# Adapter rows laid out in DRAM as the stack has them, and late loads issued in two parts, in a two-layer adapter and expert FFN kernel

## What is computed

```python
# layer 1: W 512x512; adapter of rank 16, picked per tile from 32 slots
y = x @ W.T + b + 2.0 * (x @ A[slot[t]]) @ B[slot[t]]
# layer 2: A2 64x512, router 16x512, experts B2 16x512x64
hidden = y @ A2.T
probs = softmax(y @ router.T)
topw, topi = top_k(probs, 2); topw /= topw.sum() + 1e-6
delta = sum_over_experts(weight[e] * hidden @ B2[e].T)
out = x + y @ W2.T + b2 + 0.5 * delta
```

## Time and profile before

| what | value |
|---|---|
| three runs, median (lowest to highest) | 116.63 us (116.54 to 117.41) |
| the profiled execution, its own time | 116.34 us |
| its span, first to last instruction | 114.6 us |
| so, around the span | 1.74 us |
| mean granted clock of TensorE in it | 0.955 of 2.4 GHz |
| busy share: TensorE, VectorE, ScalarE, POOL | 90%, 55%, 34%, 17% |
| bytes moved by DMA | 17.68 MB, mean 154 GB/s |

### The profile page before, as it was taken

One profiled execution on the slowest core, in us unless ns is written; L12 is line 12 of the kernel. 1 busy time (PEld: TensorE's weight loads), 2 busy tenths in 40 slices (PEclk: granted clock), 3 DMA queues, 4 the chain that ended last, 5 costly groups with the idle time before them and its releaser, 6 DMA issues.

```text
span 114.6 us, 1787 instructions
## 1 busy us (share of the span) xinstructions
PE 103.5 (90%) x577; PEld 92.8 (81%) x577; DVE 62.9 (55%) x170; ACT 38.9 (34%) x90; POOL 19.6 (17%) x33
## 2 busy tenths in 40 slices
PE   5999999998608999983999999999999999999990
PEld 5799999997508999972789879978988878878990
DVE  0465997916305234619977269309963966473211
ACT  3226726952401453306363143206241162121000
POOL 3000080000590079200620600600000000000000
PEclk9999999999995589999589999999999999999999
DMA  3899599917897112256210621283664365420211
GB/s 94 224 356 361 141 335 363 373 28 239 300 381 280 50 51 61 74 126 160 71 51 21 192 67 51 54 238 104 185 156 127 116 176 139 147 79 12 92 52 46
DMA packets 8009, 17.68 MB, mean 154 GB/s; under 512 B 1327, under 2 KB 3759, under 8 KB 7744
## 3 DMA queue, kind: packets, MB, share of 16 engines
q1 hardware_dynamic: 6126, 11.05, 32.7%
q10 hardware_dynamic: 1874, 6.51, 15.7%
HBM read 14.34 MB, written 2.77 MB: 149 GB/s over the span
## 4 chain that ended last, share of the span: by engine, by line
PE 75%; DMA 10%; issue 5%; DVE 2%; ACT 2%; SPq 2%; ACTq 2%; DVEq 0%
PE pair L711 72%; DMA spill<-w_raw_all 4%; DMA w_raw_all<-spill 3%; DMA w_raw_all<-w_cat 3%; PE pair L827 1%; SPq L242 1%; PE pair L829 1%; PE pair L818 1%; ACTq L426 1%; DVE c_lo L584 1%; DVE w_lo_all L660 1%; DVE exp_raw_all L653 1%; PE pair L838 1%; ACT c_hi L419 1%; ACT w_hi_all L474 1%
## 5 line engine op out<-in xcount | busy, mean ns | idle before, releaser
L711 PE MATMUL pair<-e_hi,w_hi_all 128*128 128x512 f32 (+1 forms) x72 | 28.0, 388 | 2.3 <-DVE w_lo_all L660 2.3
L711 PE MATMUL pair<-e_lo,w_hi_all 128*128 128x512 f32 (+1 forms) x72 | 27.2, 378 | 0.0
L711 PE MATMUL pair<-e_hi,w_lo_all 128*128 128x512 f32 (+1 forms) x72 | 27.0, 376 | 0.0
L711 PE MATMUL pair<-p_hi,x_hi 128*128 128x304 f32 x64 | 21.0, 329 | 0.0
L711 PE MATMUL pair<-p_lo,x_hi 128*128 128x304 f32 x64 | 20.3, 318 | 0.0
L711 PE MATMUL pair<-p_hi,x_lo 128*128 128x304 f32 x64 | 20.3, 317 | 0.0
L711 PEld LDWEIGHTS pair<-e_hi,w_hi_all 128*128 128x128 f32 x72 | 13.8, 192 | 5.3 <-ACT w_hi_all L474 2.6
L474 ACT ACTIVATE w_hi_all<-exp_raw_all 128x512 fp32r<-128x512 f32 x16 | 9.8, 631 | 20.5 <-DVE exp_raw_all L653 20.5
L653 DVE TENSOR_TENSOR exp_raw_all<-w_raw_all 128x512 f32<-128x512 f32 x16 | 10.8, 714 | 10.5 <-DMA w_raw_all<-spill 10.5
L711 PEld LDWEIGHTS pair<-e_hi,w_lo_all 128*128 128x128 f32 x72 | 13.9, 193 | 2.7
L711 PEld LDWEIGHTS pair<-e_lo,w_hi_all 128*128 128x128 f32 x72 | 13.8, 192 | 1.8
(11 more groups left out here) (80 smaller groups left out, 131.5 us busy)
## 6 DMA issues: line engine op xcount, KB each, us to landing
w_raw_all<-spill SPq DMA_DIRECT2D x16, 256.0 KB, 3.8
exp_raw_all<-experts ACTq DMA_DIRECT2D x4, 512.0 KB, 6.5
out<-xn SPq DMA_DIRECT2D x7, 256.0 KB, 3.7
w_raw_all<-w_cat SPq DMA_DIRECT2D x3, 552.0 KB, 6.5
xn<-x_n ACTq DMA_DIRECT2D x1, 1536.0 KB, 10.5
c_stack<-c_spill SPq DMA_DIRECT2D x14, 74.0 KB
xt_raw<-x_t ACTq DMA_DIRECT2D x1, 1024.0 KB, 7.4
xt_raw<-x_t SPq DMA_DIRECT2D x1, 512.0 KB, 8.4
```

The costliest lines, as they stand in the source:

```text
L711: return nc.tensor.matmul(out_ap, lhs, rhs, start=first, stop=last)
```

## The change

`c_spill` becomes (tile, rank, 4, columns): each row is written with its copy (both DMAs write each source row twice, so 592 KB each), and one DMA per tile reads 64 contiguous rows. The stack's row order becomes rank-major (row = 4·rank + part), and `h_stack` and tile 0's copies follow it with a stride of 4. All seven reads are issued before `spread_routing(0)`. The loads of x are issued later and in parts: x of tiles 4 to 7 and the residual of tiles 2 and 3 after `lora_t(0)`, the residual of tiles 4 to 7 after `g_hi(0, 1)`. The biases are loaded by SP's queue, ahead of x of tiles 0 and 1. On VectorE the first bias product moves behind the low parts of w, and the low parts of x of tiles 0 and 1 behind those of the folds.

```diff
-        c_spill = nc.dram_tensor("c_spill", (2, NT, R, W2N), F32, kind="Internal").ap()
+        c_spill = nc.dram_tensor("c_spill", (NT, R, 4, W2N), F32, kind="Internal").ap()
...
-        in_xn = [sem("in_xn_first"), sem("in_xn_rest")]
+        in_xn = [sem("in_xn_first"), sem("in_xn_next"), sem("in_xn_rest")]
...
@@ SP's queue @@
                 load_w(k)
+            sp.dma_start(b1_col[:, :], b1).then_inc(in_b, 16)
+            sp.dma_start(b2_row[:, :], b2).then_inc(in_b, 16)
             sp.dma_start(xt_raw[:, 0:2, :], x_t[:, 0:2, :]).then_inc(in_xt[0], 16)
...
-                    sp.dma_start(c_stack[n * R:(n + 1) * R, 0, :].bitcast(F32),
+                    sp.dma_start(c_stack[n:HR:4, 0, :].bitcast(F32),
                                  part[0:R, :].bitcast(F32)).then_inc(stacked[0], 16)
-            def stack(t):
-                for n in range(2):
-                    sp.dma_start(c_stack[2 * n * R:2 * (n + 1) * R, t, :].bitcast(F32),
-                                 c_spill[n, t].unsqueeze(0).to_broadcast([2, R, W2N])).then_inc(stacked[t], 16)
-
             sp.wait_ge(c_spilled, 32)
-            for t in range(1, 4):
-                stack(t)
+            for t in range(1, NT):
+                sp.dma_start(c_stack[0:HR, t, :].bitcast(F32),
+                             c_spill[t].rearrange("r m n -> (r m) n")).then_inc(stacked[t], 16)
...
-            spread_routing(0)
-            for t in range(1, NB):
+            for t in range(NB):
                 spread_routing(t)
-                stack(2 * t + 2)
-                stack(2 * t + 3)
...
@@ ScalarE @@
-            act.dma_start(b1_col[:, :], b1).then_inc(in_b, 16)
-            act.dma_start(b2_row[:, :], b2).then_inc(in_b, 16)
...
-                act.dma_start(c_spill[n].rearrange("t r n -> (t r) n"),
-                              part[:, :].bitcast(F32)).then_inc(c_spilled, 16)
-
-            act.dma_start(xt_raw[:, 4:NT, :], x_t[:, 4:NT, :]).then_inc(in_xt[2], 16)
-            act.dma_start(xn[:, 2:NT, :], x_n[:, 2:NT, :]).then_inc(in_xn[1], 16)
-            h_parts = h_stack[:, 0:HR].rearrange("p (a b r) -> p a b r", a=2, b=2)
+                act.dma_start(c_spill[:, :, 2 * n:2 * n + 2, :].rearrange("t r a n -> (t r) a n"),
+                              part[:, :].unsqueeze(1).to_broadcast([P, 2, W2N]).bitcast(F32)
+                              ).then_inc(c_spilled, 16)
+            h_parts = h_stack[:, 0:HR].rearrange("p (r a b) -> p a b r", a=2, b=2)
...
             lora_t(0)
+
+            act.dma_start(xt_raw[:, 4:NT, :], x_t[:, 4:NT, :]).then_inc(in_xt[2], 16)
+            act.dma_start(xn[:, 2:4, :], x_n[:, 2:4, :]).then_inc(in_xn[1], 16)
             x_hi_part(2)
...
             g_hi(0, 1)
+            act.dma_start(xn[:, 4:NT, :], x_n[:, 4:NT, :]).then_inc(in_xn[2], 16)
             lora_hi(4)
...
@@ VectorE @@
-            bias_part_of(0)
             for k in range(1, KC):
...
-            for k in range(1, KC):
+            for k in range(KC):
                 bias_part_of(k)
...
+            folded_lo(0)
+            dve.wait_ge(bph_done, 1)
+            nc.vector.tensor_tensor(bp_lo[:, :], bias_part[:, :], bp_hi[:, :].bitcast(F32),
+                                    ALU.subtract).then_inc(bpl_done, 1)
+            folded_lo(1)
+            dve.wait_ge(lbh_done, 1)
+            nc.vector.tensor_tensor(lb_lo[:, :, :].rearrange("p k (t r) -> p t k r", t=NT),
...
+                                    ALU.subtract).then_inc(lbl_done, 1)
+            for n in range(2, KC):
+                folded_lo(n)
             for t in range(2):
                 dve.wait_ge(xh_done, t + 1)
                 nc.vector.tensor_tensor(x_lo[:, t].rearrange("p k n -> p (k n)"), xt_raw[:, t, :],
...
-            dve.wait_ge(bph_done, 1)
-            nc.vector.tensor_tensor(bp_lo[:, :], bias_part[:, :], bp_hi[:, :].bitcast(F32),
-                                    ALU.subtract).then_inc(bpl_done, 1)
-            folded_lo(0)
-            dve.wait_ge(lbh_done, 1)
...
-                                    ALU.subtract).then_inc(lbl_done, 1)
-            for n in range(1, KC):
-                folded_lo(n)
...
-            h_parts = h_stack[:, 0:HR].rearrange("p (a b r) -> p a b r", a=2, b=2)
+            h_parts = h_stack[:, 0:HR].rearrange("p (r a b) -> p a b r", a=2, b=2)
...
-                dve.wait_ge(in_xn[0 if t < 2 else 1], 16)
+                dve.wait_ge(in_xn[min(t // 2, 2)], 16)
...
@@ TensorE @@
-                pe.wait_ge(stacked[t], 64 if t == 0 else 32)
+                pe.wait_ge(stacked[t], 64 if t == 0 else 16)
```

More of the change, by code:

```diff
@@ L562, in split_experts_lo @@
                                         ALU.subtract).then_inc(el_done, 1)
+            folded_lo(0)
[5 more added lines that the diff above has]
+            nc.vector.tensor_tensor(lb_lo[:, :, :].rearrange("p k (t r) -> p t k r", t=NT),
+                                    lora_raw[:, :, KC * R:AL].rearrange("p t (k r) -> p t k r", k=KC),
+                                    lb_hi[:, :, :].rearrange("p k (t r) -> p t k r", t=NT).bitcast(F32),
+                                    ALU.subtract).then_inc(lbl_done, 1)
+            for n in range(2, KC):
+                folded_lo(n)
             for t in range(2):
@@ L568, in _ @@
                                         ALU.subtract).then_inc(xl_early, 1)
-            dve.wait_ge(bph_done, 1)
-            nc.vector.tensor_tensor(bp_lo[:, :], bias_part[:, :], bp_hi[:, :].bitcast(F32),
-                                    ALU.subtract).then_inc(bpl_done, 1)
-            folded_lo(0)
-            dve.wait_ge(lbh_done, 1)
-            nc.vector.tensor_tensor(lb_lo[:, :, :].rearrange("p k (t r) -> p t k r", t=NT),
-                                    lora_raw[:, :, KC * R:AL].rearrange("p t (k r) -> p t k r", k=KC),
-                                    lb_hi[:, :, :].rearrange("p k (t r) -> p t k r", t=NT).bitcast(F32),
-                                    ALU.subtract).then_inc(lbl_done, 1)
-            for n in range(1, KC):
-                folded_lo(n)
             dve.wait_ge(bh_done, 1)
```

## The result

The changed kernel took 112.68 us in the median (111.96 to 116.75, 4 runs) against 117.02 for the kernel before (116.54 to 118.33, 4 runs). The ratio is 0.962, 95% interval 0.952 to 0.972. The forecast was 107.0 us with a range up to 111.5, so the direction was right and the size was not: 3.8% instead of 8%. The profiled execution took 113.04 us, its span is 111.2.

A forecast was written before the change was run, and what follows sets the result against it. TensorE's chain was the bound, with two breaks and a half clock after each. Experts 7.8 us earlier and 1.8 from the clock took 116.34 to 106.7; 0.3 to the median gave 107.0, range 104.8 to 111.5 including A's.

The forecast's parts named there:

- (e): Stack reads: seven issues on SP's queue, `stack(1)` slightly late; +0.5 us on TensorE, bounds 0 and +2.5.
- (f): Second break, before tile 0's experts: sixteen engines let the spill land in 2.4 us; experts at 45.7 instead of 53.46.
- Rival C: Merged stack read stays on two engines, tile 0's spill lands 6.7 us later; slower, 123.3 us, chance 0.04.
- POOL's 0.6: Allowance before tile 0's experts for POOL's low parts of x running late; 0.6 us, bounds 0 and 1.2.
- (d): Clock after the first break: no fall to half, -3.0 us up to `routing_transpose(0)`; bound 0.
- (g): Clock after the second break: no fall with a wait under 1 us, -1.8 us; bound 0.
- (c): First break: `c_lo` copies land sooner, `lora_product(0)` at 31.2 instead of 34.76, -3.55 us; bounds 30.6 and 33.
- (b): VectorE's new order: adapter product starts 0.85 us later, bounds 0 and +1.3; the later bias chain is hidden.
- (a): Biases on SP's queue ahead of x of tiles 0 and 1: 0 us, bounds -0.3 and +0.4.
- B: Queues share fairly, so the first break and its half clock stay and only the second goes; 113.4 us, chance 0.07.
- A: Wait moves to `stack(1)` or tile 0's spill behind the megabytes, clock falls after it; 110.8 us, chance 0.26.

The follow-up runs named there:

- e2: The changed kernel with `c_spill` written once and each row doubled by the read instead; 108.95 us, ratio 0.941.
- e3: The changed kernel with `c_spill` written once and the first two late loads issued after `exps(0)`; 110.79 us, ratio 0.957.
- e10: e7 with the last 1 MB residual load cut in two on SP's queue, behind the read backs of tiles 1 and 2; 107.25 us, ratio 0.917.
- e7: e2 with the first late loads on SP's queue behind `stack(3)`, and `stack(4)` to `stack(7)` behind the first two `spread_routing`; 109.16 us, ratio 0.946.
- e11: e10 with VectorE's low bias part ahead of `folded_lo(0)` and the low adapter part right behind it; 106.81 us, ratio 0.910.
- e1: The changed kernel with its first two late loads issued after `exps(0)`; 113.32 us, scattered from 111.19 to 115.33.
- e9: The changed kernel with VectorE's low bias part ahead of `folded_lo(0)` and the low adapter part right behind it; 111.94 us, ratio 0.960.
- e5: The changed kernel with VectorE's order as in the kernel before; 117.01 us, ratio 1.012.
- e12: The changed kernel with the old `c_spill` layout and its fourteen reads at their old places; 118.66 us, ratio 1.019.
- e6: The kernel before with only the late loads moved to their new places; 117.89 us, ratio 1.010.
- e4: The changed kernel with the 1 MB and 1.5 MB loads put back right behind `c_spill`; 119.56 us, ratio 1.028.
- e8: e7 with VectorE's order as in the kernel before, biases still on SP's queue; 114.81 us, ratio 0.992.

## Why the prediction was wrong

**The layout, terms (e) and (f): right in mechanism.** Sixteen engines took the place of two, the stretch at 0.13 went, and TensorE's own 9.5 us became the bound from the routing transpose on. Rival C is refuted. That tile 0's spill landed in 1.4 us (2.4 foretold) is in part luck. The reads and loads were priced at 386 GB/s and to be through at 37.3; they ran at about 200 and were through near 41.3, still ahead of a spill that the first break had put off to 42.88. Where nothing puts it off, the spill takes 3.0 us (e2) to 7.19 (e3). POOL's 0.6 was not needed in the changed kernel; that the half clock in front left it its slack is likely, and no run isolates it.

**The clock, terms (d) and (g).** The second fall went, worth 1.5 us and not 1.8: the three first matmuls take 0.94 at full clock as well (e10), and 1.62 at half (e3). The first fall stayed, since its break stayed. Its price was right: from `lora_product(0)` to the routing transpose there are 7.09 us in the changed kernel and 4.16 in e10, where nothing falls (4.0 foretold). In e7, e10 and e11, where neither product waits, the clock row has no fall at all; in e2 it falls behind the wait of `lora_product(1)` instead.

**The first break, term (c): the step that failed.** It took the megabytes to be gone from in front of the copies and put the wait before the product at 0.6 us (30.6 to 31.2); the wait was 4.97 and the product at 35.35. The price taken was 1.2 MB of writes at 386 GB/s, and the second copy's issue at 28.1. In the changed kernel DMA moved 244 and 208 GB/s in the two microseconds from 28 to 30 (shares 1.12 and 0.81), the issue was held from 28.07 to 30.21, and by then the loads of 28.82 and 29.20 stood in front. I had taken a place behind in program order for a place behind in the transfers. The error of 4.4 us in the wait divides by e1: without the loads 1.90 us of wait are left where the changed kernel has 4.97 and e9, with its loads too, 5.09, so 3.1 are the loads', and 1.3 are the doubled writes' above the price I had put on them. With the single write the wait is gone even with the loads in place (e2).

From there the sum closes on the profiled execution, 113.04 us against 106.7. The product was 4.15 us late. The fall of the clock, less the 0.5 that I had for `stack(1)`, brings the routing transpose to 42.44 instead of 35.7, 6.7 late. From there to the transpose of tile 4 there are 10.16 us where the sum has 10.0 up to the experts and 0.6 for their first three matmuls, so 0.4 comes back. That leaves 6.3, the whole error.

**The order on VectorE, term (b): near in size, wrong on what is hidden.** The adapter product was at 21.74, 0.62 later than before, not 0.85. The bias chain, which I had called hidden behind the first fold, is itself on the chain that ended last:

```profile
3.85 7.48 DMA w_raw_all<-w_cat
...
16.75 0.85 DVE bias_part L535
...
17.62 0.70 ACT bp_hi L398
18.32 0.56 ACT p_hi L380
```

ScalarE makes `bp_hi` first and the fold's `p_hi` behind it. So the adapter product starts 10.41 us behind the last part of the weights, 11.33 to 21.74, and in e7 again, 10.17 to 20.58; there it is earlier than the 21.12 of the kernel before. Of those 10.41 the place of the low bias part is 0.5 (e11). I also missed what the move buys. I costed the biases on SP's queue (term (a)) at 0, and that holds only with the bias product moved too: e5 is 1.012 where the change is 0.962. Whether the pair gains anything with the new layout is open, since no run undoes both moves; with the old layout it gained nothing (e12 with both is 1.019, e6 with neither 1.010).

**The rivals.** B has nearly the number, 113.4, and names what stayed (the first break and its half clock), but for the wrong reason: it had the queues share fairly. The runs speak against that: with 1.5 MB or more issued in front, 8 KB took 3.1 us (e7) to 7.2 (e3) against 1.4 undisturbed, and 148 KB 7.1 (e2) to 10.0 (e4) against 2.6 to 3.1 for `stack(1)` to `stack(3)` in e7, where the loads are behind them. The Trainium skill ("DMA: Bandwidth & Descriptors", "Queues, rings and completion order") says that an engine takes turns between its queues by packets. Where the loads were on the other queue than the small transfer, the runs show no quick passage by that: 6.26 us (e1), 7.12 (e2), 7.19 (e3). In e7 both are on one queue, so it is no test of it. A was right about the kind, a small transfer behind the megabytes. In the changed kernel that was the copy, and not `stack(1)` or the spill, which A named; those came up as soon as the copy was free (e2, e1, e3). The forecast itself, 107.0, is what e10 and e11 reach (107.25 and 106.81), with the experts of tile 0 at 46.44 in e10 where 45.7 was foretold; it takes both the single write and the loads kept away from every small transfer.

**The parts of the change.** All but the loads' move 1.028 (e4), all but the layout 1.019 (e12), all but VectorE's order 1.012 (e5), the loads' move alone 1.010 (e6), together 0.962. None of the three can be left out: the layout needs the loads out of the way, and the loads' new place only pays where the reads behind it use all engines. The layout was not run on the old biases and the old order of VectorE.

What stays open is why an issue is held. It was with the doubled write (2.08 to 2.50 us for the second copy in the changed kernel, e1, e4, e5 and e9) and not with the single one (e2, e3, e6, e7, e8, e10, e11, e12), but the kernel before also had one stack read of 2.45 us in the earlier trace rows beside its loads, so the doubled write is one way to it and not the only one. No run varied the number of rows in flight alone.

## What to carry to other kernels

Follow every small transfer on the chain (a copy, a spill, a read back) and ask which large load was issued in front of it on any queue, in issue time and not in program order; moving one load moves the wait to the next small transfer, so place all loads against all of them at once, here behind the small ones on the same queue and cut in parts. Look at the slowest dimension of a DMA on both sides, and at a DMA share near 2/16 over a long stretch; duplicate rows by a repeat inside the read, not in the write. When a load moves behind others, look for what waits for it first on its consumer's engine, and move that too.

## What the runs showed of the hardware that was not expected

- Sixteen engines at a full share moved 204 GB/s with the reads of rows of 2368 bytes alone (35.7 to 36.7 us in e2), and 386 GB/s with the loads of x: a full share is no rate.
- An issue on SP's queue of 0.6 us can take 2.14 us while DRAM writes of two times 592 KB are in flight, and ScalarE's next issue then took 1.43 instead of 0.46.
- A bias row of 2 KB, issued behind the weights, landed 6.0 us after issue (e5).
- Three matmuls of 512 columns that follow a wait are shown as 0.94 us at full clock too (e10), and as 1.62 at half (e3), so the 0.94 in the earlier trace rows was no sign of the lower clock.
- The length of a wait alone does not tell whether the clock falls behind it. It fell behind waits of 1.90 us (e1, in front of the product), 2.6 (e2) and 3.0 (e3); it did not behind 1.6 (e10), 2.1 (e11) and 2.60 (e1, in front of the experts).
